# Spectral bins half a step higher, their matrices in eight chunks, and the tail of each scan window weighed on TensorE and ScalarE

## What is computed

```
h[n, s] = exp(dt[s] * A[n]) * h[n, s-1] + (dt[s] * u[s]) * B[n, s]
y[s]   += sum over n of h[n, s] * C[n, s]
```

```
U_plus  = irfft(rfft(phi) * rfft(u));   U_minus = the same of u * (-1)^t, times (-1)^t
out     = sum over k of (U_plus[k] * s[k]) @ Mpp[k] + (U_minus[k] * s[k]) @ Mpm[k] + short causal terms
```

## Time and profile before

| | |
|---|---|
| runs shown | 9278.6, 9300.02 and 17873.6 us; median 9300.02 |
| the profiled execution | 9263.69 us; span 9261.9 us |
| PE busy | 7254.6 us (78%), mean granted clock 0.896 |
| DVE busy | 6461.8 us (70%) |
| ACT busy | 4717.5 us (51%) |
| POOL busy | 4250.9 us (46%) |
| scan stage, four batches | to about 4224 us |
| spectral stage | about 4224 to 6007 us |
| later layers | from there to the end |

### The profile page before, as it was taken

How to read it: one execution, slowest core, us unless ns; L and a number is a source line. 1 busy time by engine, 2 the same in 40 slices (tenths; PEclk the granted TensorE clock), 3 DMA queues, 4 the chain that set the end, 5 groups by cost and what they waited for, 6 DMA issues and landing times. The chain is left out here.

```text
span 9261.9 us, 165385 instructions
## 1 busy us (share of the span) xinstructions
PE 7254.6 (78%) x63005; PEld 4679.2 (51%) x63005; DVE 6461.8 (70%) x8039; ACT 4717.5 (51%) x8987; POOL 4250.9 (46%) x3064
## 2 busy tenths in 40 slices
PE   5777778777777778774789999568479999996576
PEld 3444434443444444443778887357345555553354
DVE  7999899997999899994156565232366666553447
ACT  4666566665666466663156565223224444454335
POOL 4999589994999599993300000000100000010005
PEclk8999999999999999996699999789769999998678
DMA  4555355553555355553432324631310000103010
GB/s 146 164 166 164 95 172 164 166 164 100 165 166 164 91 177 164 165 162 109 162 90 60 87 73 103 143 98 39 138 36 16 22 16 22 32 1 147 14 34 21
DMA packets 471266, 976.50 MB, mean 105 GB/s; under 512 B 128184, under 2 KB 226943, under 8 KB 453375
## 3 DMA queue, kind: packets, MB, share of 16 engines
q1 hardware_dynamic: 469490, 938.16, 34.1%
q10 hardware_dynamic: 960, 27.53, 1.1%
HBM read 822.11 MB, written 114.81 MB: 101 GB/s over the span
## 5 line engine op out<-in xcount | busy, mean ns | idle before, releaser
L892 POOL TENSOR_TENSOR ss_work<-ss_dtu,ss_ringb 128x768 f32<-128x768 f32 x1536 | 2761.5, 1824 | 259.1 <-POOLq L59 255.6
L754 PE MATMUL ss_ps<-ss_work,ss_ident 128*128 128x512 f32 (+1 forms) x6144 | 2309.6, 522 | 628.8 <-POOL ss_work L902 601.1
L754 PEld LDWEIGHTS ss_ps<-ss_work,ss_ident 128*128 128x128 f32 x6144 | 1198.2, 203 | 1521.0 <-issue 1319.3
L876 DVE TENSOR_TENSOR_SCAN ss_work<-ss_ps,ss_last,ss_work 128x768 f32<-128x768 f32 x1024 | 1811.3, 1804 | 67.6 <-ACT ss_ps L807 56.8
L807 ACT ACTIVATE ss_ps<-ss_dt,ss_a_neg 128x768 f32<-128x768 f32 x1536 | 1374.6, 895 | 289.0 <-DVE ss_work L876 272.0
L861 DVE TENSOR_TENSOR ss_work<-ss_work,ss_ps 128x1152 f32<-128x1152 f32 x768 | 1021.6, 1330 | 1.2 <-ACT ss_ps L815 1.2
L2658 DVE TENSOR_REDUCE at_top<-at_ps 128x1 f32<-128x384 f32 x1512 | 728.4, 547 | 400.1 <-PE at_ps L2576 399.9
L2639 ACT ACTIVATE at_probs<-at_ps 128x768 f32<-128x768 f32 x864 | 653.7, 808 | 657.7 <-PE at_ps L2595 656.8
L876 DVE TENSOR_TENSOR_SCAN ss_work<-ss_ps,ss_work 128x768 f32<-128x768 f32 x512 | 878.9, 1745 | 50.6 <-issue 17.5
L1409 DVE COPY mb_mix<-mb_ps 128x432 f32<-128x432 f32 x1088 | 633.7, 631 | 390.1 <-PE mb_ps L1432 389.9
L1499 ACT ACTIVATE mb_mix<-mb_ps 128x432 f32<-128x432 f32 x1088 | 613.0, 619 | 444.9 <-PE mb_ps L1432 439.0
(11 more groups left out here) (558 smaller groups left out, 9743.2 us busy)
## 6 DMA issues: line engine op xcount, KB each, us to landing
ss_ringb<-scan_rows SPq DMA_DIRECT2D x768, 384.0 KB, 3.6
ss_ringc<-scan_rows SPq DMA_DIRECT2D x768, 384.0 KB, 3.9
c_w<-in_l_ffn_w SPq DMA_DIRECT2D x52, 1024.0 KB, 12.6
mb_mats<-fq_mats ACTq DMA_DIRECT2D x8, 3360.0 KB, 16.5
at_packs<-at_high SPq DMA_DIRECT2D x64, 288.0 KB, 5.5
fq_mats<-fq_mats_high SPq DMA_DIRECT2D x8, 2048.0 KB, 9.2
fq_bins<-tb_out SPq DMA_DIRECT2D x68, 216.0 KB, 1.9
mb_bins_by<-fq_bins SPq DMA_DIRECT2D x34, 432.0 KB, 3.7
```

What stands on the lines that cost most here:

```text
L754: return pe.matmul(acc[:, d * WIN + a:d * WIN + e], ident[:, :], weighed[:, t % DEEP, d, a:e], start=n == 0 and e - a == 512, stop=n == NS ...
L876: dve.tensor_tensor_scan(hid[:, t % DEEP, d, ::step], decay[d][:, ::step], drive[:, t % DEEP, d, ::step], start, ALU.mult, ALU.add).then_i ...
L892: pool.tensor_tensor(drive[:, t % DEEP, d, :], dtu[:, t // NST % 2, d, :], ringb[:, t % RING, :], ALU.mult).then_inc(s["driven"], 1)
```

## The change

*Scan.* The window is cut in three instead of two: DVE weighs positions 0 to 512, POOL 512 to 640, and the last 128 (TAIL = 640 to 768) are turned by PE: two transposes per state (`turn_tails`) put positions on partitions, where C is one number per partition; ACT copies the result out of PSUM with C as its scale (`scale_tails`); PE adds it to the sums as the stationary operand against the identity, which turns it back (`add_tail`). C of the three tails is turned once per batch (`c_turned`). `copy_c` is one copy of 512 columns instead of two of 512 and 64. PE's order of sums changes so that all that needs DVE's share alone comes first, then the transposes of the next state, then POOL's share, then the tails.

*Spectral unit.* The frequencies of each segment are moved by half a bin, so that no bin is its own mirror: SEG_SLOTS = (48, 24, 12, 9), 16 + 8 + 4 + 3 = 31 trios, 93 slots. The turned filters and x have 128 rows (ROWS_K) instead of 100 (rows without content are zero). The filters' part of `to_bins` and `branch_weights` become `taps_to_bins`, which runs ahead of the norm while x is loaded, and rounds each filter's taps in one copy instead of two. The summing and splitting of the matrices goes from POOL to DVE and ACT, in five pieces between the copies of bins. In `mix_bins` the matrices are loaded in eight chunks, each reloaded once its last use is past. `from_bins` reads 96 and 90 rows per half instead of 102 each, in four transfers per step instead of eight.

```diff
-SPLIT = 576
+SPLIT = 512
+TAIL = WIN - P
@@ scan_windows, PE
+            def turn_tails(t):
+                if t > LAST:
+                    return
+                pe.wait_ge(s["scanned"], 2 * t + 2)
+                for d in range(D2):
+                    ins = pe.transpose(tail_ps[:, d, :], hid[:, t % DEEP, d, TAIL:WIN], ident[:, :])
+                ins.then_inc(s["turned"], 1)
+
+            def add_tail(t, d):
+                return pe.matmul(acc[:, d * WIN + TAIL:(d + 1) * WIN], tails[:, t % 2, d, :], ident[:, :], start=False, stop=t % NST == NST - 1, skip_group_check=True)
+
+            for n in range(NWIN):
+                ins = pe.transpose(spread_c[:, n * P:(n + 1) * P], rowsb[:, n * WIN + TAIL:(n + 1) * WIN], ident[:, :])
+            ins.then_inc(s["c_made"], 1)
+            turn_tails(0)
             for t in range(STATES):
                 i, n = t // NST, t % NST
                 beside(t + 2)
...
+                if n == 0:
+                    turn_tails(t + 1)
                 pe.wait_ge(s["weighted"], t + 1)
-                pe.wait_ge(s["pool_weighted"], t + 1)
+                if n == 0 and i:
+                    pe.wait_ge(s["kept"], D2 * (i - 1) + 1)
+                add_weighed(t, 0, 0, 512, True)
...
-                add_weighed(t, 0, 512, WIN)
-                add_weighed(t, 1, 0, 256).then_inc(s["summed"], 1)
-                add_weighed(t, 1, 256, WIN).then_inc(s["summed"], 1)
+                add_weighed(t, 1, 0, 256)
+                add_weighed(t, 1, 256, SPLIT, True)
+                if n:
+                    turn_tails(t + 1)
+                pe.wait_ge(s["pool_weighted"], t + 1)
+                for d in range(D2):
+                    add_weighed(t, d, SPLIT, TAIL)
+                pe.wait_ge(s["scaled"], t + 1)
+                for d in range(D2):
+                    add_tail(t, d).then_inc(s["summed"], 1)
@@ scan_windows, ScalarE
-                act.activation(spread_c[:, OVER:], ringc[:, t % RING, OVER:SPLIT], ACT.Copy).then_inc(s["copied"], 1)
-                act.wait_ge(s["scanned"], 2 * t + 2)
-                act.activation(spread_c[:, 0:OVER], ringc[:, t % RING, 0:OVER], ACT.Copy).then_inc(s["copied"], 1)
+                act.activation(spread_c, ringc[:, t % RING, 0:SPLIT], ACT.Copy).then_inc(s["copied"], 1)
+
+            def scale_tails(t):
+                k, n = SECTIONS[t // NST]
+                row = NST * (k // 2) + t % NST
+                act.wait_ge(s["turned"], t + 1)
+                if t >= 2:
+                    act.wait_ge(s["summed"], 2 * (t - 2) + 2)
+                act.activation(tails[:, t % 2, :, :], tail_ps, ACT.Copy, scale=c_turned[:, n, k % 2, row:row + 1]).then_inc(s["scaled"], 1)
...
                 if t:
                     copy_c(t - 1)
+                    scale_tails(t - 1)
                 decays(t, 1)
@@ scan_windows, VectorE: weigh and scan
-                dve.wait_ge(s["copied"], 2 * t + 2)
+                dve.wait_ge(s["copied"], t + 1)
                 dve.wait_ge(s["scanned"], 2 * t + 2)
-                if t < LAST:
-                    dve.wait_ge(s["decayed"], 2 * t + 4)
...
                         dve.wait_ge(s["ended"], t - DEEP + 1)
+                        dve.wait_ge(s["turned"], t - DEEP + 1)
@@ scan_windows, GpSimd
-                pool.tensor_tensor(weighed[:, t % DEEP, :, SPLIT:WIN], hid[:, t % DEEP, :, SPLIT:WIN], bc(ringc[:, t % RING, None, SPLIT:WIN], [P, D2, WIN - SPLIT]), ALU.mult).then_inc(s["pool_weighted"], 1)
+                pool.tensor_tensor(weighed[:, t % DEEP, :, SPLIT:TAIL], hid[:, t % DEEP, :, SPLIT:TAIL], bc(ringc[:, t % RING, None, SPLIT:TAIL], [P, D2, TAIL - SPLIT]), ALU.mult).then_inc(s["pool_weighted"], 1)
@@ spectral
-SEG_SLOTS = (49, 25, 13, 9)
+SEG_SLOTS = (48, 24, 12, 9)
...
-            load_all(nc, "fq_load", [(flat[ROWS_T * (b % 2):ROWS_T * (b % 2) + ROWS_T, RES * (b // 2):RES * (b // 2) + RES, :],
+        taps_to_bins(nc, w, x_dram, ps, U, turned, fe, fa, sign, far, far_r, mats, lags, wgt, root, taps_dram)
+        norm_and_turn(nc, "fq_ln", U[:, :, :, :], U[:, :, :, :], 1e-5)
+        to_bins(nc, w, ps, U, turned, fe, fa, mats, lags, wgt, bins_dram, mats_dram)
...
+        def load_mats(eng, n, chunk):
+            part = slice(chunk * PIECE, (chunk + 1) * PIECE)
+            eng.dma_start(mats[:, part].bitcast(F32), mats_dram[n, :, part]).then_inc(chunk_loaded[chunk], 16)
...
-                        if c in BEGIN:
-                            pe.wait_ge(s[f"mats_loaded{h}"], 16 * (BEGIN[c] + 1))
+                                if c in BEGIN and n % FILLS_IN == 0:
+                                    pe.wait_ge(chunk_loaded[CHUNKS_H * h + n // FILLS_IN], 16 * (BEGIN[c] + 1))
...
-                            if c in LAST and h == 1 and stretch == 0:
-                                load_mats(LAST[c] + 1, 0)
-                    if c in LAST:
-                        act.wait_ge(s["made"], filled(c, 1, FILLS - 1) + 1)
-                        load_mats(LAST[c] + 1, 1)
+                            if c in LAST and stretch % STRETCH_IN == STRETCH_IN - 1:
+                                load_mats(act, LAST[c] + 1, CHUNKS_H * h + stretch // STRETCH_IN)
```

More of the change, by code:

```diff
@@ L420, in selective_scan_mixer @@
         size = DEEP * D2 * WIN
-        drive, hid, weighed = (part(n * size, [DEEP, D2, WIN]) for n in range(3))
+        drive, hid, weighed = (part(n * size, [DEEP, D2, width]) for n, width in enumerate((WIN, WIN, TAIL)))
         xpad, rowsb = part(0, [D2, 50, 50]), part(2 * size, [S])
@@ new lines, in _ @@
+                dve.wait_ge(s["copied"], 1)
+                dve.tensor_copy(taps[:, :, TAPS:2 * TAPS], taps[:, :, 0:TAPS]).then_inc(s["spread"], 1)
+                for n in range(TRIOS):
+                    dve.wait_ge(s["rounded"], n + 1)
+                    low = split[TAPS:2 * TAPS, n % RING_T, :]
+                    dve.scalar_tensor_tensor(low, bank(GROUPS_K + n)[TAPS:2 * TAPS, 0:COLS], root[TAPS:2 * TAPS, :], low, ALU.mult, ALU.subtract).then_inc(s["lowered"], 1)
+                dve.wait_ge(s["mats_loaded"], 32)
@@ new lines, in _ @@
+                for q in range(PIECES):
+                    raw, total_m = pieces[q][0], pieces[q][1]
+                    dve.tensor_scalar(total_m, raw, wgt[0:raw.shape[0], 0:1], None, ALU.mult).then_inc(s["summed"], 1)
+                for q in range(PIECES):
+                    dve.wait_ge(s["cut"], q + 1)
+                    dve.tensor_tensor(pieces[q][3], pieces[q][1], pieces[q][2], ALU.subtract).then_inc(s["cut_low"], 1)
+                dve.wait_ge(s["cut_low"], PIECES)
+        s.end()
@@ new lines, in to_bins @@
+def to_bins(nc, w, ps, U, turned, fe, fa, mats, lags, wgt, bins_dram, mats_dram):
+    CG = C // 8
+    RING_B = 4
+    PHASES = 4
+    flat = U[:, :, :, :].rearrange("p g t c -> p (g t) c")
+    ax = turned[:, :].rearrange("p (n r c) -> p n r c", r=2, c=C)
+    pieces = matrix_pieces(mats, lags)
+    starts = [0]
+    for ph in range(PHASES):
+        starts.append(starts[-1] + 2 * CG + PART_TRIOS[ph % 2])
+    def owner(n):
+        ph = max(p for p in range(PHASES) if starts[p] <= n)
+        v = n - starts[ph]
@@ L1580, in _ @@
                 load_taps(0)
-                load_bins(0)
+                for chunk in range(1, 2 * CHUNKS_H):
+                    load_mats(sp, 0, chunk)
+                    if chunk == CHUNKS_H - 1:
+                        load_bins(0)
                 for c in range(TRIOS):
@@ L3309, in frequency_tables @@
     for n, slots in enumerate(SEG_SLOTS):
-        around = 2 * (slots - 1)
+        around = 2 * slots
         length, rows = around * RES, np.arange(ROWS_T >> n)
```

436 lines of the change are left out of this document (224 added, 212 removed).

## The result

The changed kernel took 9663.95 us (median; 9639.05 to 9726.12), the kernel before 9289.31 us on the same chip: ratio 1.0426, 95% interval 1.0371 to 1.048, 375 us slower. (The ratio leaves out a single slow run of the kernel before, 17873.6 us; the medians count it.) The forecast was 9500, slower by 2.2%; the direction and the range held, the size was little more than half of what was measured. The profiled execution has a span of 9665.9 us, 404 more than before. I cut it where lines of the kernel stand for stages: the scan ends with the last sum onto `xb` (4223.6 before, 4812.6 after), the spectral unit with the start of the next layer's norm (6027.0 and 6424.5).

The account below looks back on a forecast made before the run. POOL was taken to bound the scan before, and a ring of waits between ScalarE and TensorE after. 9264 + 415 (scan, bounds +330 and +550) - 179 (spectral) = 9500 us, range 9300 to 9680.

Parts of the forecast that it names:

- The bound before, and the shares: Scan: POOL bounds sections of 76.9 us, DVE 2 us behind; smaller weighings save 0.27 (POOL) and 0.13 us (DVE) a state.
- The ring, plain turns: Scan: ScalarE's scaled copy waits for transposes behind TensorE's sums; a turn takes 4.91 or 5.35 us against DVE's 4.55.
- +454 for the scan: Scan: the loss in us if two transposes in a row took 0.55, from the skill's 275 ns each, instead of 0.47.
- Eleven long states 63.6 us: Scan states n = 4 to 14: six turns of 4.91, five of 5.35, plus y 4.4 and Exp or Ln 3.0.
- a section at 86.4 us with TensorE's clock as before: Scan: 63.6 us for eleven states plus 22.8 for five, instead of 76.9, in 44 sections: +418 us.
- DVE's edge costs as much; I leave both out: Scan: ScalarE's lead of up to 2.0 us a section and DVE's wait at the section's edge were taken to cancel.
- five states at 4.55: Scan: the five other states of a section run at DVE's 4.55 us each, 22.8 in all.
- The spectral stage: Stage after the scan: mixing, chunks, front, `to_bins` and `from_bins` together gain 179 us, bounds 110 and 250.
- -102 - 25: Mixing of bins: three trios fewer save 102 us, chunks reloaded early at three segment changes 25, bounds 0 and 36.
- The ring has slack: Rival in the scan: tails are turned before ScalarE needs them, sections about 74 us, both gains arrive, 8950 us; chance 0.09.
- the ring binds only where enlarged: Rival in the scan: only y, Exp or Ln lengthen turns; sections 80.2 us, +145, time 9230, no change; chance 0.07.
- TensorE's clock falls: Rival in the scan: at 1.2 GHz the ring's TensorE part doubles, +36 us a section, about 11100 us; chance 0.02.

Follow-up runs that it names:

- e7: The changed kernel without turning, scaling and adding the tails, so the last 128 positions of each window are missing from y: 8884.2 us, ratio 0.9569.
- e4: The changed kernel with five products of zeros on TensorE ahead of the step's piece, in four states a section behind an Exp or Ln: 9658.9 us.
- e5: The changed kernel with the adding of the old y moved behind the turning of the tails, ahead of POOL's share of the sums: 9461.9 us.
- e9: The changed kernel with its matrices still in eight chunks, but awaited and reloaded by fours: 9686.2 us, ratio 1.0428.
- e2: The scan of the kernel before with the changed spectral unit: 9122.7 us, ratio 0.983 to the kernel before.
- e3: The changed kernel with TensorE turning the next state's tails before its sums in every state, not only n = 0: 9083.3 us, ratio 0.9785.
- e6: The changed kernel with each pair of tails turned three times in a row onto the same place: 9940.6 us, ratio 1.0714.
- e10: e3 with y added in n = 7 to 12 and short products of zeros in TensorE's waits: 9056.8 us, ratio 0.9756 to the kernel before.
- e11: e3 with the same products of zeros as e10, but y in n = 5 to 10 as in the change: 9112.7 us, ratio 0.9797.

## Why the prediction was right in direction and off in size

*The bound before, and the shares.* Right: POOL 0.28 and DVE 0.14 saved a state for 0.27 and 0.13, and e7 shows that with no ring a section is 72.8, as worked out.

*The ring, plain turns.* Right to 0.01 us, 4.92 and 5.34 for 4.91 and 5.35. That it is so close is in part luck, since two terms were off and cancel: transposes and hand-over 0.42 for 0.47 + 0.04, the scaling 0.37 for 0.28 (this copy, with a scale per partition, took 0.473 us, not the 0.38 of the like one). The transposes passed 0.11 us apart in the changed kernel (524.09 to 524.31 for two). The Trainium skill's 275 ns ("TensorE: Matmul & The Clock Gate", Part 4) agrees with how long one is in flight, mean 280 ns in L759's group, but not with what another one adds; +454 for the scan would have been nearer to the result by accident.

*Eleven long states 63.6 us.* Right with the clock at its upper level: in the section of 1341 to 1428, along rows, ScalarE's exponentials give 62.5 us for eleven turns, where the prediction has 63.6 - 4.4 + 3.2 = 62.4, and in e4 the mean of all 44 sections is 63.57. Exp, Ln and y stand rightly in it (e5).

*The step that failed first: a section at 86.4 us with TensorE's clock as before.* I took the clock as all or nothing ("it was granted 0.96 there"), gave a full fall 0.02 and a partial one nothing. The mean stayed 0.96, and still single states at the lower level cost 2.0 us a section, 89 in all: those behind a wait of 2.1 us, which the ring itself creates by Exp and Ln, and whose slow part lies wholly in the ring. The eleven turns took 65.59 us where 63.6 was forecast, and 63.57 once the waits were filled (e4).

*The second: "DVE's edge costs as much; I leave both out" and five states at 4.55.* The five other states took 24.80 us instead of 22.8: 2.0 a section, 88 in all. At the edge the ring binds as well, with two states of sums ahead of the transposes. I had looked only for rings in states with a job. With no tails (e7) the five take 22.6. The lower level has a part in the 2.0 too, since it is there in all 44 sections; how much is its and how much the ring's at the upper level no run separates. Together, by the sections, that is (90.3 - 86.4) x 44 = 172 of the 174 us missing. It put the scan above my own bound of 550.

*The spectral stage.* -191.5 for -179. The mixing's -127 is what -102 - 25 gave, though by e9 the 25 is rather 12 to 22. The wait before the first fill fell by 13.3 for the 13 forecast, 8.9 of it by the chunks. Up to the first fill -59 for -47, but wrongly placed: the front did not gain 22 but lost 45.5, since the taps' work outlasts the loading of x, and the stretch from the norm on gained 105. Part of that is the clock's: from the norm to the first product other kernels with the same code took 1 to 63 us more than the 313.6 of the changed kernel, and e2 alone gained 160 us where the trace of the change promised 191. That the stage came so near its forecast is therefore luck in part: over the ten kernels it gained 121.5 to 191.5 us against the trace of before. `from_bins` -5.4 for -5.

*Rivals.* "The ring has slack" is refuted by e3 and e6, "the ring binds only where enlarged" by the plain turns at 4.92. "TensorE's clock falls" was right as a mechanism and wrong as a case by itself: it belonged inside the forecast as a term. The number of transposes does not show in it: over the same 200 us (400 to 600) the granted clock was 0.97 with three times as many (e6) and 0.95 with none (e7), where the change has 0.96.

## What to carry to other kernels

With engines that run in order, draw the ring before you count load: from an instruction that now waits, back through each queue to the engine itself, and sum one turn with everything that stands between. If a turn is longer than the bound's share per state, smaller shares elsewhere are worth nothing, and moving one short instruction ahead of a long one in another queue can be worth more than the whole change (here 581 us). Look for the ring also at the edges of a loop, and count a wait that a ring makes on TensorE twice: once for itself, once for the clock behind it.

## What the runs showed of the hardware

- TensorE's granted clock falls within single states of a busy scan: 128x512 sums and pieces behind a wait of 2.1 us took 2.48 and 1.02 us instead of 1.89 and 0.70, and the next such wait had no such effect (1641.04). The Trainium skill (same page, Part 1) tells of a kernel whose clock goes to and fro with short waits between groups of matmuls; this trace agrees. Products of zeros in the waits kept the clock at the upper level behind them in all 44 sections of e4, e10 and e11 (1.00 over 200 us in e10), not at the edges, where none stood in the wait for the old sums.
- The same stretch of the same code, from the norm to the first fill, took 297.5 us at a granted clock of 0.74 and 360.8 at 0.58; differences of 50 us between two traces of this kernel can be that alone.
- A copy of 128x256 out of PSUM on ScalarE took 0.473 us with a scale per partition and 0.383 without; the pace was 0.37 and 0.28.
